# Three of four channel groups of delta and of its product with x on GpSimd, with their store one step later

## The reference, cut to what matters

```python
delta = jax.nn.softplus(jnp.einsum('blr,dr->bld', dt, W_dt) + b_dt)
A = -jnp.exp(A_raw)

def step(h, inp):
    x_t, dlt, B_t, C_t = inp
    dA = jnp.exp(dlt[:, None, :] * A[None])
    h = dA * h + dlt[:, None, :] * B_t[:, :, None] * x_t[:, None, :]
    y_t = jnp.einsum('bn,bnd->bd', C_t, h) + D * x_t
    return (h, y_t)
```

## Time and profile before

| | us |
|---|---|
| median of 3 runs | 3724.76 (3722.89 to 3726.68) |
| the profiled execution | 3729.7 |
| its span | 3727.9 |
| busy: TensorE, VectorE, ScalarE, GpSimd | 3214.2, 2150.3, 1581.5, 648.1 |
| `scan`, `out`, `into` on VectorE, 128 each | 566.2, 290.3, 292.7 |

### The profile page before, as it was taken

The page is one execution under the profiler, slowest core; times in us unless marked ns, Lnnn a source line. Parts: engine busy times, 40 slices in busy tenths (PEclk is TensorE's granted clock), DMA queues, the critical chain, the costliest instruction groups (busy, mean ns, idle before and its releaser), DMA issues. The chain is left out here.

```text
span 3727.9 us, 40912 instructions
## 1 busy us (share of the span) xinstructions
PE 3214.2 (86%) x12812; PEld 1764.7 (47%) x12813; DVE 2150.3 (58%) x2698; ACT 1581.5 (42%) x3074; POOL 648.1 (17%) x767
## 2 busy tenths in 40 slices
PE   7688888878888852699889999999999999987996
PEld 5344443534344410366534444444444444436775
DVE  2299999999999989322214344444444443433334
ACT  3466566565656542133222324242324242423443
POOL 0000202020211202133200202020202020206772
PEclk8898989889898975799989999999999999988998
DMA  2345454655555464422120101010101010046557
GB/s 62 86 108 147 133 159 119 161 142 139 151 135 152 129 168 132 167 66 66 67 92 1 56 1 56 1 56 1 56 1 56 3 54 3 30 169 191 157 157 265
DMA packets 193227, 362.86 MB, mean 97 GB/s; under 512 B 28274, under 2 KB 85106, under 8 KB 191922
## 3 DMA queue, kind: packets, MB, share of 16 engines
q1 hardware_dynamic: 164514, 296.19, 27.8%
q0 software_dynamic: 20352, 57.17, 4.2%
q10 hardware_dynamic: 8208, 7.54, 0.6%
HBM read 250.53 MB, written 110.28 MB: 97 GB/s over the span
## 5 line engine op out<-in xcount | busy, mean ns | idle before, releaser
L1646 DVE TENSOR_TENSOR_SCAN hs<-dA,hs 128x2048 f32<-128x2048 f32 x128 | 566.2, 4423 | 16.1 <-ACT dA L1489 9.1
L453 POOL COPY rows<-slot 128x64 f32<-128x64 f32 x48 | 18.6, 417 | 2652.9 <-DVE new_pl L590 2611.5
L2236 PE MATMUL ps<-pT,V 128*128 128x512 f32 x1024 | 450.7, 593 | 0.9 <-DVE pT L2404 0.9
L1489 ACT ACTIVATE dA<-dl,w_An 128x511 f32<-128x511 f32 x512 | 326.7, 711 | 173.4 <-DVE hs L1646 162.0
L1337 PE MATMUL ps<-hs,w_S 128*32 128x512 f32 x1024 | 173.5, 723 | 181.9 <-DVE hs L1652 181.9
L1638 DVE TENSOR_TENSOR hs<-u,bb 128x2048 f32<-128x2048 f32 x128 | 292.7, 2287 | 58.0 <-issue 37.1
L2236 PEld LDWEIGHTS ps<-pT,V 128*128 128x128 f32 x1024 | 189.9, 190 | 220.8 <-issue 214.4
L1652 DVE TENSOR_TENSOR hs<-hs,cb 128x2048 f32<-128x2048 f32 x128 | 290.3, 2269 | 0.0
L1806 POOL DMA_INDIRECT slots<-og,idt x232 | 241.8, 1042 | 258.9 <-DVE og L1894 196.9
L449 POOL DMA_INDIRECT sorted<-rows,new_pl x192 | 274.6, 1430 | 63.6 <-issue 44.8
L2311 ACT ACTIVATE pp<-ps,nm 128x512 f32<-128x512 f32 x256 | 172.3, 685 | 215.1 <-DVE nm L2387 215.1
(11 more groups left out here) (353 smaller groups left out, 5406.1 us busy)
## 6 DMA issues: line engine op xcount, KB each, us to landing
bb<-bcd SPq DMA_DIRECT2D x128, 256.0 KB
cb<-bcd SPq DMA_DIRECT2D x128, 256.0 KB
dl<-dld SPq DMA_DIRECT2D x128, 256.0 KB, 6.7
u<-ud SPq DMA_DIRECT2D x128, 256.0 KB, 7.9
xg<-sorted SPq DMA_DIRECT2D x232, 136.0 KB, 2.1
slots<-zeros SPq DMA_DIRECT2D x136, 128.0 KB, 7.8
qrg<-slots SPq DMA_DIRECT2D x32, 512.0 KB, 16.3
rg<-slots SPq DMA_DIRECT2D x32, 256.0 KB, 4.8
```

The source lines that it names most:

```text
L1489: act.activation(m.dA[:, N % 2, q, 1:T], m.dl[:, G % 2, q, 1:T], ACT.Exp, scale=An[:, e, N % GROUP:N % GROUP + 1]).then_inc(s_da, 1)
L1646: dve.tensor_tensor_scan(state, m.dA[:, N % 2].rearrange("p j t -> p (j t)"), state, 0.0, ALU.mult, ALU.add).then_inc(s_h, 1)
L2236: ins = pe.matmul(ps[:, 6 + j, :], V[:, m, h * D + j * P:h * D + (j + 1) * P], pT[:, i % 2, h % 2, m, :], start=(h == 0 and m == 0), stop= ...
```

## The change

`delta_ready` on VectorE keeps only group 0 of the two operations. Groups 1 to 3 of both are done by GpSimd in a new function, `other_deltas`, 128 x 1536 each, which waits for the same semaphores. The store of groups 1 to 3 waits for GpSimd and is issued in step 15 and not in step 14, behind the reads of group 0. On ScalarE the decays of the next batch's first step are written ahead of `scale_turned` in step 15.

```diff
         def delta_ready(dve, m, c, k):
             dve.wait_ge(m_pre, JI * (k + 1))
             dve.wait_ge(m_ln, k + 1)
-            dve.tensor_tensor(c.dl, c.pre, c.ab, ALU.add).then_inc(m_dlr, 1)
+            dve.tensor_tensor(c.dl[:, 0, :], c.pre[:, 0, :], c.ab[:, 0, :], ALU.add).then_inc(m_dlr, 1)
             dve.wait_ge(m_dlr, k + 1)
-            dve.tensor_tensor(c.u, c.dl, m.xs[:, :, :], ALU.mult).then_inc(m_u, 1)
+            dve.tensor_tensor(c.u[:, 0, :], c.dl[:, 0, :], m.xs[:, 0, :], ALU.mult).then_inc(m_u, 1)
+
+        def other_deltas(pool, m, c, k):
+            pool.wait_ge(m_pre, JI * (k + 1))
+            pool.wait_ge(m_ln, k + 1)
+            pool.tensor_tensor(c.dl[:, 1:, :], c.pre[:, 1:, :], c.ab[:, 1:, :], ALU.add).then_inc(m_dlg, 1)
+            pool.wait_ge(m_dlg, k + 1)
+            pool.tensor_tensor(c.u[:, 1:, :], c.dl[:, 1:, :], m.xs[:, 1:, :], ALU.mult).then_inc(m_ug, 1)
...
-        def store_groups(sp, c):
+        def store_groups(sp, c, k):
+            sp.wait_ge(m_ug, k + 1)
             sp.dma_start(dld[1:JI].rearrange("j p t -> p j t"), c.dl[:, 1:JI, :]).then_inc(m_st, 16)
             sp.dma_start(ud[1:JI].rearrange("j p t -> p j t"), c.u[:, 1:JI, :]).then_inc(m_st, 16)
...
                             if n == 14 and kc is not None:
                                 store_first_group(sp, c, kc)
-                                store_groups(sp, c)
                                 spread_delta(sp, m, JI * kc, range(GROUP))
                                 spread_u(sp, m, JI * kc, range(GROUP))
+                            if n == 15 and kc is not None:
+                                store_groups(sp, c, kc)
...
                             if kc is None and n in (0, 1, 2, 11, 12, 13, 14, 15):
-                                sp.wait_ge(m_u, B)
+                                sp.wait_ge(m_ug, B)
...
-                    for k in range(B - 1):
-                        send_rows_in_turn(pool, M0, v, k)
-                        pool.wait_ge(M0.listed, 16 * TT * M0.K * (k + 1))
+                    other_deltas(pool, m, c, 0)
+                    for b in range(B):
+                        k, kc = behind(b), next_up(b, 1)
+                        if k is not None:
+                            send_rows_in_turn(pool, M0, v, k)
+                            pool.wait_ge(M0.listed, 16 * TT * M0.K * (k + 1))
+                        if kc is not None:
+                            other_deltas(pool, m, c, kc)
...
                         elif n == 15:
+                            if kc is not None:
+                                decays_ahead(1)
                             if ke is not None:
                                 scale_turned(act, c, ke, 0, 0)
-                            if kc is not None:
-                                decays_ahead(1)
                             if ke is not None:
                                 scale_turned(act, c, ke, 0, 1)
                             decays_ahead()
```

More of the change, by code:

```diff
@@ L394, in build @@
         m_dlr, m_u = sem("mix_delta_ready", stage), sem("mix_input_ready", stage)
+        m_dlg, m_ug = sem("mix_other_deltas_ready", stage), sem("mix_other_inputs_ready", stage)
         m_bst = sem("mix_bc_stored", stage)
@@ L1270, in _ @@
                     spread_u(sp, m, 0, range(GROUP))
-                    store_groups(sp, c)
+                    store_groups(sp, c, 0)
                     spread_delta(sp, m, 1, range(GROUP))
```

## The result

| | median us | range |
|---|---|---|
| before | 3725.32 | 3722.89 to 3726.68, 4 runs |
| after | 3769.34 | 3765.17 to 3770.81, 4 runs |
| ratio | 1.0117 | 95% interval 1.01 to 1.0135 |

The account below looks back on a forecast made before the run. VectorE was taken as the bound. GpSimd +23.8, waits for u -5.7, late stores +7.2, start 0 sum to +25.3 us: 3755.0 on the profiled 3729.7, stated as 3750 us against the median 3724.76; range 3726 to 3770.

Parts of the forecast that it names:

- case D: Whole kernel: the change turns out as forecast, 3738 to 3761 us; chance 0.61.
- rival C: GpSimd operations up to 4.7 us (about 3772), or late stores 3 us a batch (3761); both 3782; chance 0.15.
- GpSimd beside VectorE: Step 13: GpSimd costs VectorE 6.6 us a batch, VectorE sheds 3.2; net 3.4, seven batches +23.8 us.
- into(16): Batch's first `into`: its six waits for u's last read vanish once reads precede the store, -5.7 us.
- late stores: Steps 15 to 17: stores land about 505.5, `add_state(14)` ends 513.5, `into(17)` waits 1.2 us six times, +7.2 us.
- start: Batch 0: u of group 0 ready at 150.9, as now (150.75), 0 us; up to +3.3 if GpSimd goes first.
- Exclusion both ways: `delta_ready`: two-input VectorE and SBUF-reading GpSimd instructions block each other, 3.3 us per GpSimd operation.
- Rival A: `delta_ready`: two-input operations do not exclude each other for long, GpSimd works beside VectorE; -22.9, 3702 us; chance 0.12.
- Rival B: `delta_ready`: GpSimd at its floor, 1.57 + 0.15 us twice, 3.4 a batch against 3.2; 3722 to 3730; chance 0.12.
- The two passes of 1.02 ns a column: GpSimd's two-input operation reads its inputs one after another, 1.02 ns per column each: 3.14 us for 1536 columns.
- at more than 4 (C): Sign in the trace: GpSimd's rows in `delta_ready` at more than 4 us would speak for rival C.
- The decays: Step 15 on ScalarE: step 16's decays, moved ahead of `scale_turned`, cost nothing and gain nothing.

Follow-up runs that it names:

- gpsimd_one_input: The changed kernel with GpSimd's two operations on groups 1 to 3 replaced by one-input copies, results not valid: 3757.45 us, ratio 1.0075.
- gpsimd_writes_only: The changed kernel with GpSimd's two operations on groups 1 to 3 replaced by memsets that read nothing, results not valid: 3757.3 us, ratio 1.0078.
- store_behind_reads: The changed kernel with the store of groups 1 to 3 in step 14, right behind group 0's reads and ahead of C and B: 3748.83 us, ratio 1.0049.

## Why the prediction was right, and what it mis-sized

The forecast was slower, 3750 us in 3726 to 3770; measured are 3769.34. Direction and mechanisms are as named; the size is 19 us off. That it lies inside the range, by 0.7 us, is in part luck. It is not in the 3738 to 3761 of case D, the change as forecast (0.61), but where rival C (0.15) has late stores at 3 us a batch or more. And 12.7 us that no term counts came back in steps 2 to 4; without them it would have been about 3782. Forecast and trace by the terms of the sum, in us (what is in none of them cancels, -2.1 in batch 0, +1.6 in batch 7 and +0.4 in the six between):

```
term                          forecast   measured
GpSimd beside VectorE, seven     +23.8      +21.9   (step 13)
into(16), six                     -5.7       -6.3   (step 15)
late stores, six                  +7.2      +25.5   (steps 0, 2, 3 and 4)
start                              0         +0.6
sum                              +25.3      +41.7 up to the last scan, +41.2 in the span
```

- **Exclusion both ways: right.** Each of the pair is held 3.26 and 3.13 us (3.94 and 3.81 less 0.68) where 3.3 was forecast, and `gpsimd_one_input` and `gpsimd_writes_only` show that GpSimd's reading is the cause. Rival A would have needed `into` and the pair at their own durations beside GpSimd. Rival B's floor of 1.57 us is nearer to the copy (1.81 us long, VectorE held 1.26) than to the two-input operation.
- **The two passes of 1.02 ns a column: right** for the time that VectorE is held by two inputs. The working fits less well: a copy holds it 1.26 us and not the 1.57 of one pass, so the second input costs more than the first. The rows of GpSimd, 3.66 to 5.36 us, contain GpSimd's own wait for VectorE, so "at more than 4 (C)" was a bad sign to look for: some are at 4.9 and VectorE still loses only 3.2. The Trainium skill (GPSIMD Engine Reference, section "Elementwise — side-by-side cycle accounting") led to an estimate of 3.37 us; the trace has 3.1 to 3.3 held.
- **`into(16)`: right.** Step 15 is at 8.91 us in batches 1 to 6.
- **The decays: not contradicted.** ScalarE's `scale_turned` is released by the DMA 11.78 us after its last work, so the decays ahead of it do not delay it. No run moves them alone.
- **The start: right, in its way too.** VectorE's addition is not held (0.69 us), its multiplication is held by GpSimd's addition, and u of group 0 is ready at 151.12, where 150.9 was forecast and 150.75 was before. The reads are issued 0.35 us later, the first `into` starts 0.69 and the first scan 0.59 us later. That `into` waits 9.48 us and not 12.38 is no earlier landing: `gated_ready` in front of it is itself held by GpSimd, 4.43 us in place of 1.22.

```profile
147.31 3.81 DVE L994 TENSOR_TENSOR W0u<-W0u,xs 128x512 f32<-128x512 f32 x1
151.04 4.43 DVE L978 TENSOR_TENSOR W0u<-x,W0u 128x1024 f32<-128x1024 f32 x1
164.96 2.29 DVE L1653 TENSOR_TENSOR hs<-u,bb 128x2048 f32<-128x2048 f32 x1 [9.48 <-DMA u<-ud]
```

- **The late stores: mechanism right, size wrong.** The step that failed is "The same 16 us of DMA work, now from 489.5 with the stores last, put their landing at about 505.5". From u ready to landing it allowed 19.1 us, and it was 23.4. The sum of the work was the same, but not what stands ahead of the store: C and B now do, they run at a quarter of the DMA engines' share, and the store ends behind them. `store_behind_reads`, in which they don't, took 17.5 us. The chain behind the landing, 8.0 us to the end of `add_state(14)`, was right (514.85 to 522.69 are 7.8), and so was the way to `into(17)`: 1.2 us and 4.3 more make 5.5, and it waits 5.53 in batch 2. Over six batches step 0 grew by 38.2 us, and 12.7 came back in steps 2 to 4, mostly because `into(20)` no longer waits (2.4 to 3.5 us before, at most 0.43 after); the prediction named that wait, but only as room in which lateness of TensorE would vanish, and counted no return. Net 4.2 a batch, which is what rival C put at 3. Two of its signs failed with this term: the batch period is 174.3 us and not 171.6, and `into(17)` waits 4.6 to 6.6 us and not about 1.

The rest of the 19 us is the zero: before's profiled execution was 4.9 us above the median used, after's 1.5 above its own. The profiled times alone are 3770.8 against 3755.0 forecast, 16 us apart. Most of that is the stores' 18.3 less the exclusion's 1.9.

## What to carry to other kernels

Before giving part of a two-input VectorE operation to GpSimd, compare what each column frees and what it blocks: here 1.0 ns freed and about 2 ns blocked. By that no share of it would gain while VectorE is busy with two-input work; one and three groups of four were tried, and both lose. A store that others wait for should be costed with everything that the new place puts ahead of it in the queue, small broadcasts included, and on the DMA engines that these use, not by its bytes. And where a wait is the release of a whole queue, moving one waiting instruction ahead mostly renames it: three kernels here did so, two got back 0.2 to 0.3%, and none was faster than the kernel before.

## What the hardware showed that I had not expected

- A broadcast of four rows to 128 partitions runs at a DMA share of 0.26 and 98 to 102 GB/s, while full-width stores move 375 to 409 GB/s at a share of 1.02 to 1.05. With the eight reads and two such broadcasts ahead of them, the two large stores had landed 17.6 us after the issue of the last read (497.11 to 514.7); with the reads alone ahead of them, 11.7 (493.67 to 505.4). Writing the broadcast with another outermost dimension was not tried.
- GpSimd's memset of 128 x 1536 runs in 1.38 us beside VectorE's two-input products (all sixteen take 1378 to 1384 ns), and neither holds the other, where a copy of that size costs VectorE 1.26 us.
- GpSimd gets in between two queued VectorE instructions each time. In `store_behind_reads`, as in batches 3 and 4 of the change, it came in one boundary earlier, and `into` itself was held:

```profile
476.73 4.51 POOL L999 TENSOR_TENSOR W0u<-W0u 128x1536 f32<-128x1536 f32 x1 [9.82 <-ACT W0u L965]
...
477.84 5.55 DVE L1652 TENSOR_TENSOR hs<-u,bb 128x2048 f32<-128x2048 f32 x1
```

Which boundary it takes makes no difference to the sum: 5.55 - 2.29 is 3.26 us again.
